# A distance-attention loop: clips in halves, logarithms by single blocks, rounding on ScalarE

## The reference

```
P = X @ W_in + b_in            # X: layer norm of x; per head 64 columns each of Q, K, V, G
d2 = sum(Q*Q) + sum(K*K) - 2 * Q @ K.T
W  = (1e-4 + sqrt(max(d2, 0))) ** -2
W  = W / (1e-4 + sum(W, axis=-1))
H  = G * (W @ V)
```

## Time and profile before

| | |
|---|---|
| median of 3 runs | 1581.67 us (1579.9 to 1582.06) |
| profiled execution | 1582.67 us, span 1580.8 us |
| TensorE | 1420.2 us busy (90%) |
| VectorE | 1045.0 us (66%) |
| ScalarE | 927.3 us (59%) |
| GpSimd | 648.9 us (41%) |
| attention over distances | from the start to about 905 us |

### The profile page before, as it was taken

The page is one execution under the profiler, slowest core; times in us unless marked ns, Lnnn a source line. Parts: engine busy times, 40 slices in busy tenths (PEclk is TensorE's granted clock), DMA queues, the critical chain, the costliest instruction groups (busy, mean ns, idle before and its releaser), DMA issues. The chain is left out here.

```text
span 1580.8 us, 23151 instructions
## 1 busy us (share of the span) xinstructions
PE 1420.2 (90%) x7425; PEld 902.6 (57%) x7426; DVE 1045.0 (66%) x1406; ACT 927.3 (59%) x646; POOL 648.9 (41%) x484
## 2 busy tenths in 40 slices
PE   6899999999999999999998569999984799999995
PEld 4555555555555555554554157777764566676664
DVE  7878998889888988898887726666665322222221
ACT  1879888988998899889989602222221122222221
POOL 5255456545554555455543512212220233333331
PEclk9899999999999999999999879999995899999998
DMA  4000000000000000000000313111120134233312
GB/s 145 14 1 15 27 27 13 13 27 27 13 13 27 27 13 13 27 27 13 7 14 14 113 40 109 44 42 53 46 81 14 22 87 139 35 82 81 88 30 70
DMA packets 67483, 66.90 MB, mean 42 GB/s; under 512 B 5152, under 2 KB 59936, under 8 KB 67424
## 3 DMA queue, kind: packets, MB, share of 16 engines
q1 hardware_dynamic: 60160, 56.58, 11.0%
q0 software_dynamic: 7296, 9.97, 3.8%
HBM read 48.70 MB, written 19.92 MB: 43 GB/s over the span
## 5 line engine op out<-in xcount | busy, mean ns | idle before, releaser
L1630 POOL TENSOR_TENSOR v_aug<-v_aug,wts 128x1024 f32<-128x1024 f32 x96 | 254.8, 2654 | 250.1 <-ACT wts L1483 245.5
L998 DVE TENSOR_SCALAR wts<-ps_s,k 128x1024 f32<-128x1024 f32 x240 | 297.2, 1280 | 85.4 <-PE ps_s L538 64.5
L1475 ACT ACTIVATE wts<-wts 128x4096 f32<-128x4096 f32 (+1 forms) x80 | 231.8, 2935 | 88.5 <-DVE wts L998 68.8
L553 PE MATMUL ps_o<-wts,g_r 128*64 128x512 f32 x1024 | 251.4, 614 | 11.3 <-ACT wts L1483 11.2
L1481 ACT ACTIVATE wts<-wts,eps_d 128x4096 f32<-128x4096 f32 (+1 forms) x80 | 241.5, 3019 | 0.2
L1483 ACT ACTIVATE wts<-wts 128x4096 f32<-128x4096 f32 (+1 forms) x80 | 235.1, 2939 | 2.5
L1396 DVE TENSOR_TENSOR wts<-rinv,ps_s 128x352 f32<-128x352 f32 x76 | 39.6, 521 | 253.7 <-ACT rinv L1548 170.6
L793 PE MATMUL ps_s<-wts,qk 128*128 x608 | 197.9, 469 | 3.1 <-issue 2.3
L987 DVE TENSOR_TENSOR v_aug<-v_aug,wts 128x1024 f32<-128x1024 f32 x96 | 156.1, 1626 | 5.4 <-ACT wts L1483 5.1
L538 PE MATMUL ps_s<-q_hi,k_hi 64*128 64x512 f32 x512 | 115.8, 446 | 40.3 <-DVE wts L998 30.1
L793 PEld LDWEIGHTS ps_s<-wts,qk 128*128 128x128 f32 x608 | 110.6, 192 | 64.6 <-issue 16.8
(11 more groups left out here) (240 smaller groups left out, 2425.2 us busy)
## 6 DMA issues: line engine op xcount, KB each, us to landing
wts<-in_w SPq DMA_DIRECT2D x16, 704.0 KB, 5.4
h_t<-o_raw SPq DMA_DIRECT2D x16, 512.0 KB, 2.6
qk<-h_t SPq DMA_DIRECT2D x16, 512.0 KB, 4.1
wts<-in_w SPq DMA_DIRECT2D x8, 640.0 KB, 7.1
raw_qk<-in_w_in SPq DMA_DIRECT2D x32, 128.0 KB, 2.2
raw_vg<-in_w_in SPq DMA_DIRECT2D x32, 128.0 KB, 2.2
acc<-wts SPq DMA_DIRECT2D x17, 128.0 KB, 1.7
wts<-in_x SPq DMA_DIRECT2D x2, 1024.0 KB, 6.0
```

The costliest lines, as they stand in the source:

```text
L553: mm = pe.matmul(ps_o[r, t], v_pair[:, b, r], wts[:, h, b, t], start=b == 0, stop=b == SB - 1)
L998: dve.tensor_scalar(wts[:, h, b, :], ps_s[:, h, :], k2[:, 2 * b + h:2 * b + h + 1], 0.0, ALU.add, ALU.max).then_inc(S_.max_ok, 1)
L1475: act.activation(chunk(start, end), chunk(start, end), ACT.Sqrt).then_inc(S_.sqrt_ok, 1)
L1630: pool.tensor_tensor(acc_w[:, 0], acc_w[:, 0], wts[:, 0, b], ALU.add).then_inc(S_.add_ok, 1)
```

## The change

Blocks 0, 2 and 4 of pairs 1 to 15 go through the clips in two halves of 512 queries: TensorE signals after the first half of the distances (`fill_s`), VectorE clips that half for both heads and signals `fill_ok`, and TensorE may then write the first half of the next block while the second half is clipped. `LOGS` has seven chunks in place of five: blocks 2, 3, 4 and 5 go one by one. `split_high` leaves VectorE's list and goes to ScalarE's, between the roots of block 6 and block 7; there it waits for the copies of q and k and for all distances of the pair that still read the old rounded parts.

```
-LOGS = ((0, 1), (1, 2), (2, 4), (4, 6), (6, 8))
+LOGS = ((0, 1), (1, 2), (2, 3), (3, 4), (4, 5), (5, 6), (6, 8))
+HALVED = (0, 2, 4)
 def distances(n, b):
-    elif not fill:
+    elif not fill and b - 1 not in HALVED:
         pe.wait_ge(S_.max_ok, NB * n + 2 * b)
     for th in range(2):
+        if not fill and b - 1 in HALVED:
+            if th == 0:
+                pe.wait_ge(S_.fill_ok, SB + len(HALVED) * (n - 1) + HALVED.index(b - 1) + 1)
+            else:
+                pe.wait_ge(S_.max_ok, NB * n + 2 * b)
...
-        if fill:
+        if fill or b in HALVED and th == 0:
             mm.then_inc(S_.fill_s, 1)
 def guard(n, b, free):
+    if b in HALVED:
+        dve.wait_ge(S_.fill_s, 2 * SB + len(HALVED) * (n - 1) + HALVED.index(b) + 1)
+        if free is not None:
+            dve.wait_ge(S_.add_ok, free)
+        t = slice(0, HALF)
+        for h in range(2):
+            g = dve.tensor_scalar(wts[:, h, b, t], ps_s[:, h, t], k2[:, 2 * b + h:2 * b + h + 1], 0.0, ALU.add, ALU.max)
+        g.then_inc(S_.fill_ok, 1)
     dve.wait_ge(S_.s_ready, SB * (n - 1) + b + 1)
     if free is not None:
         dve.wait_ge(S_.add_ok, free)
+    if b in HALVED:
+        t = slice(HALF, 2 * HALF)
+        for h in range(2):
+            dve.tensor_scalar(wts[:, h, b, t], ps_s[:, h, t], k2[:, 2 * b + h:2 * b + h + 1], 0.0,
+                              ALU.add, ALU.max).then_inc(S_.max_ok, 1)
+        return
 # VectorE, pair
-    if ahead == 2:
-        split_high(p + 2)
 # ScalarE
+def split_high(n):
+    act.wait_ge(S_.q_ok, n + 1)
+    act.wait_ge(S_.s_ready, SB * (n - 1))
+    act.activation(q_hi[:], q32[:], ACT.Copy)
+    act.wait_ge(S_.k_cp, n + 1)
+    act.activation(k_hi[:], k32[:], ACT.Copy).then_inc(S_.hi_ok, 1)
+def roots(n, ahead=False):
     for start, end in ROOTS:
+        if ahead and end == SB:
+            split_high(n + 1)
```

More of the change, by code:

```diff
@@ L1467, in rows @@
                 act.activation(rinv[:], rinv[:], ACT.Exp, scale=-1.0).then_inc(S_.r_ok, 1)
-            def roots(n):
+            def split_high(n):
[5 more added lines that the diff above has]
+            def roots(n, ahead=False):
                 for start, end in ROOTS:
-                    if isinstance(n, int) and start in (2, 4):
+                    if ahead and end == SB:
+                        split_high(n + 1)
+                    if isinstance(n, int) and n == 0 and start in (2, 4):
                         turned_high(start + 2)
@@ L1488, in _ @@
             weights(0, True)
-            with act.Fori(1, PAIRS) as p:
-                roots(p)
+            with act.Fori(1, PAIRS - 1) as p:
+                roots(p, ahead=True)
                 weights(p, False)
+            roots(PAIRS - 1)
+            weights(PAIRS - 1, False)
             rows(PAIRS - 1)
```

## The result

The changed kernel takes 1588.54 us (median of 13 runs, 1586.83 to 1591.53), the kernel before 1581.87 us in the 13 runs beside it. The ratio is 1.0047, with a 95% interval from 1.0036 to 1.0058: slower by 6.7 us, under 1%, but clear of no change by the interval. Forecast were 1589.0 us and slower. The profiled execution took 1587.25 us, with a span of 1585.4.

What follows compares the result with a forecast made beforehand. The bound was the loop over pairs: ScalarE's last exponential, then six alternating GpSimd and VectorE instructions. 0.54 us more a pair gives 7.0 over 13 periods, edges +0.4: 1590.1 profiled, median 1589.0 us (+0.47%); range 1570 to 1594, its own 1585 to 1594.

Steps and rivals of the forecast that it cites:

- The sum: One pair, first logarithm to the next: terms along ScalarE, GpSimd and VectorE add to 53.56 us, against 53.02 before.
- The 0.86 us for two more splits: ScalarE, splitting two double chunks of logarithms: some 0.86 us more work, uncovered, ahead of the last exponential.
- t = 32.52: Time in us from a pair's first logarithm (t = 0) at which ScalarE's last exponential was forecast to end.
- the 0.32 us wait at the copy of k: VectorE's copy of k waited 0.32 us for a projection; forecast to go, as the projection is then ready.
- The line of six: GpSimd's adds 6, 7 and square of q, VectorE's add 5, gate product and add 6, without a gap: 9.93 us.
- The bound that VectorE could come 2.3 us later for nothing: VectorE could reach add 5 up to 2.3 us later without changing when the six two-operand instructions end.
- The waits ahead of distances 6 and 7: TensorE: new waits of some 1.5 us each at distances 6 and 7.
- The idle time ahead of the last root: ScalarE, after its two rounding copies: some 0.7 us idle left before the last root.
- The rival in which ScalarE alone sets the pace: The six come apart and ScalarE's own work bounds the loop: 51.6 us a pair, near 1563 us; chance 0.10.
- One meeting less: VectorE's add 5 is over before GpSimd's add 6 starts: period 52.4 us, near 1574 us; chance 0.11.
- The extra meeting at the copy of k: VectorE's add 7 loses to GpSimd's square of k and waits 1.9 us: near 1614 us; chance 0.05.
- The edges: Loop ends: pair 0 keeps a 0.8 us lead, last preparation and last pair cost +1.2; together +0.4 us.

Runs made afterwards that it cites:

- chunks_alone: The kernel before with the seven chunks of logarithms as the only edit: 1590.93 us, ratio to before 1.0058.
- old_chunks: The changed kernel with the five old chunks of logarithms, halves and rounding on ScalarE kept: 1573.41 us, ratio to before 0.9944.
- square_early: The changed kernel with GpSimd's square of q moved ahead of its add of block 6: 1577.43 us, ratio to before 0.9969.
- all_single: The changed kernel with blocks 6 and 7 as single chunks too, eight in all: 1563.57 us, ratio to before 0.9888.
- no_halves: The changed kernel with no block halved, seven chunks and rounding on ScalarE kept: 1590.47 us, ratio to before 1.0054.
- single_alone: The kernel before with eight single chunks of logarithms as the only edit: 1591.89 us, ratio to before 1.0052.
- late_single: The changed kernel with chunks (0,1), (1,2), (2,4), (4,6), (6,7), (7,8), so only the last double chunk is split: 1594.0 us, ratio to before 1.0068.
- single_round_vector: The changed kernel with eight single chunks and the rounding back on VectorE: 1574.13 us, ratio to before 0.9944.

## Why the prediction was right

*The period.* The mechanism held: ScalarE's last exponential releases the line, and the period is the sum from there. The sum forecast 53.56 and the trace gives 32.52 + 0.16 + 9.79 + 0.20 + 2.39 + 5.08 + 0.03 + 3.23 = 53.40. The 0.86 us for two more splits came out to the hundredth (t = 32.52; the terms printed beside it make 0.88), and the 0.32 us wait at the copy of k went. The line of six was taken at 9.93 and took 9.79: VectorE's add 5, which had waited, ended 1.10 us after GpSimd's (528.10 to 529.20), where the earlier trace rows had 1.21 for one that had not waited. With 0.01 from each of two other terms this is the mis-sized part: 0.37 us a pair more than before, where I had 0.54, and 4.7 us over 13 pairs in place of 7.0.

*Where the loss comes from.* chunks_alone has all of it, old_chunks has none, and taking either of the two other edits out of the changed kernel moves the period by 0.01 us at most. Together, without the chunks, they gained 0.47 on the kernel before (old_chunks), which the prediction, pricing them beside the chunks only, did not say. That the line hangs on ScalarE's last exponential is shown from both ends: 0.86 us less there shortened the period by 0.83 (old_chunks), with the line as long as in the changed kernel (9.80 against 9.79), and taking the square out of the line shortened it by 0.88 with all seven chunks in place (square_early).

*What hides the rest.* The bound that VectorE could come 2.3 us later for nothing held for the halves and for the rounding, as far as they test it: in chunks_alone VectorE comes latest, 0.7 us later than in the changed kernel. The waits ahead of distances 6 and 7 were forecast at 1.5 us each and come to 7.9 / 6 = 1.3. The idle time ahead of the last root was forecast at 0.7 and is 0.79.

*The rivals.* The rival in which ScalarE alone sets the pace is the truth of another kernel: all_single, at 51.71 us a pair. The 51.6 that I had given this state is near it in part by luck, as it was for seven chunks: the eighth adds 0.4 us, and the roots and copies took some 0.3 less than I had counted. One meeting less did not happen in the changed kernel, since VectorE was 0.17 us late for it. The extra meeting at the copy of k did not occur; VectorE's add 7 still lasts as long as a free one.

*The edges.* These were off. Pair 0 gained 1.94 us (119.87 to 117.93) and not 0.8. The load ahead of the logarithms of pair 0 stands at 62.90 us here and 62.87 before, so this gain lies in pair 0 itself. It takes 55.03 us from that load to the next in the changed kernel and 57.43 in no_halves (64.41 to 121.84), so the halves give 2.4 us there, where I had counted only the wait at distances 1. The other 1.5 of the 3.9 us between 121.84 and 117.93 were there at the load of pair 0 already, ahead of every block that this edit touches; four other profiles have it between 64.2 and 64.6 too, and the rest between 62.6 and 62.9. The cause of that was not looked for. From pair 14 on the changed kernel loses again. Its first product of the output projection stands at 913.4 us against 909.8, so the loop as a whole cost 3.6 us: -1.9 from pair 0, +4.7 from 13 periods, +0.8 from the last pairs. Another 1.0 of the 4.6 us between the spans comes after it, in code that the change does not touch. The medians differ by 2.1 us more than the spans: the profiled execution was 1.3 below its median here and 0.8 above it before.

*The luck.* The forecast of 1589.0 is nearer to the measured 1588.54 than its parts deserve. The period was 2.3 us too high, and the edges of the loop were 1.5 too high as well (+0.4 forecast, -1.1 measured). What brought the total back is the 1.0 behind the loop and the 2.1 between profiled and median times, for which the forecast had no term; another 0.2 is that the kernel before had a median of 1581.87 beside the changed one and 1581.67 in the forecast. The direction and the mechanism are not luck; the last half microsecond is.

## What to carry to other kernels

Where VectorE and GpSimd both run instructions with two SBUF operands, look for a stretch in which they alternate without a gap: in this kernel it behaved as one serial resource, its length was near the sum over both engines (9.79 us, against 2 x 2.39 + 1.89 + 3 x 1.21 = 10.3 for the six without a wait), and what VectorE or TensorE gained ahead of it was lost in it. What counts is when its first instruction is released and how many are queued behind. Splitting the producer's last chunk, so that the first of them starts earlier, was worth 25 us on top of the changed kernel, while splitting the earlier chunks alone cost 9. But the same split was worth 14 with the rounding on VectorE, nothing on the kernel before with seven chunks (single_alone beside chunks_alone, 0.4 us a pair longer), and with the old double chunks ahead of it it cost 21 (late_single beside old_chunks). So it is no rule by itself. After such an edit compare who starts first at each meeting: a lead of 0.2 us or less can decide over 2 us of one instruction and nearly 1 us of the period.

## What the runs showed that I had not expected

Who goes first is settled by tenths of a microsecond, and in late_single by hundredths. GpSimd's 0.12 us lead in single_round_vector and VectorE's 0.22 us lead in all_single are 0.34 us apart and make 0.88 us a pair. A periodic loop need not be periodic under this: late_single has pairs of 53.1 and of 54.6 us in one execution, with the same instructions, and which it is follows the order at one add. And ScalarE's copies with rounding took 1.04 us when they followed one another without a wait and 1.06 when the first had waited.
